# Two of four query and key projections moved behind the values and behind the base linear, each pair with its own tiles for the natural layout

## The reference

```
xn = layernorm(x)
q = (xn @ Wq.T + bq)      # 32 heads of 16, per head 1024 x 16
k = (xn @ Wk.T + bk)
v = (xn @ Wv.T + bv)
att = softmax(causal(q @ k.T / 4))
attn_out = (att @ v) @ Wo.T + bo
base_out = xn @ base_W.T + base_b
w = expert weights from softmax(xn @ router_W.T + router_b), mapped by expert_map
lora = ((xn @ A.T) * w) @ B * 2
x = x + attn_out + base_out + lora
```

## Time and profile before

| | us |
|---|---|
| median of three runs | 685.1 |
| lowest and highest | 684.2 to 689.15 |
| the profiled execution, its time | 686.73 |
| the profiled execution, its span | 685.0 |
| TensorE busy in it | 622.2 (91%) |
| DVE, ACT busy | 373.4, 293.7 |
| router logits to values, stretch | 266.15 to 334.73 |
| values, stretch | 334.73 to 371.42 |
| linear, up to the first score of attention | 371.42 to 416.64 |

### The profile page before, as it was taken

One profiled execution on the slowest core, in us unless ns is written; L12 is line 12 of the kernel. 1 busy time (PEld: TensorE's weight loads), 2 busy tenths in 40 slices (PEclk: granted clock), 3 DMA queues, 4 the chain that ended last, 5 costly groups with the idle time before them and its releaser, 6 DMA issues.

```text
span 685.0 us, 9336 instructions
## 1 busy us (share of the span) xinstructions
PE 622.2 (91%) x3688; PEld 407.8 (60%) x3688; DVE 373.4 (55%) x547; ACT 293.7 (43%) x509; POOL 76.9 (11%) x106
## 2 busy tenths in 40 slices
PE   3999999999999998872998997999999999989985
PEld 3788888878888866662765664444444444333444
DVE  6676553176453275431476546678888888610025
ACT  4545333135332132121321114677777777583450
POOL 3000000000000029000000232121221211211010
PEclk9999999999999999997899997999999999795998
DMA  6332332111101111478731003253362601010003
GB/s 217 124 103 93 113 104 81 61 38 56 61 32 61 62 62 25 145 191 217 266 110 31 2 1 68 41 107 78 60 108 46 96 25 29 12 31 10 11 26 127
DMA packets 24305, 53.64 MB, mean 78 GB/s; under 512 B 8881, under 2 KB 9393, under 8 KB 24257
## 3 DMA queue, kind: packets, MB, share of 16 engines
q1 hardware_dynamic: 23972, 52.46, 28.2%
q0 software_dynamic: 288, 0.58, 0.5%
HBM read 39.77 MB, written 10.61 MB: 74 GB/s over the span
## 4 chain that ended last, share of the span: by engine, by line
PE 74%; DVE 9%; ACT 7%; DMA 6%; issue 2%; SPq 1%; POOLq 0%; POOL 0%; ACTq 0%; DVEq 0%
PE bank L1148 11%; PE bank L1131 10%; PE slot L887 8%; PE bank L887 8%; PE bank L889 7%; PE bank L888 7%; PE slot L888 7%; PE slot L889 7%; DMA heads_dram<-attn_lo 6%; PE slot L1054 5%; ACT probs L869 5%; DVE maxcol L1453 2%; PE slot L1062 2%; DMA stage<-in_stream 1%; PE slot L903 1%
## 5 line engine op out<-in xcount | busy, mean ns | idle before, releaser
L869 ACT ACTIVATE probs<-bank 128x512 f32<-128x512 f32 (+2 forms) x320 | 156.1, 560 | 70.3 <-PE bank L1131 68.6
L1453 DVE TENSOR_REDUCE maxcol<-slot 128x2 f32<-128x1024 f32 (+2 forms) x112 | 124.8, 1142 | 42.7 <-PE slot L1062 22.3
L887 PE MATMUL slot<-xt_hi,ring_hi 128*128 128x512 f32 (+2 forms) x248 | 99.9, 403 | 21.7 <-DVE attn_lo L1409 18.2
L889 PE MATMUL slot<-xt_hi,ring_lo 128*128 128x512 f32 (+2 forms) x248 | 98.8, 399 | 0.0
L888 PE MATMUL slot<-xt_lo,ring_hi 128*128 128x512 f32 (+2 forms) x248 | 98.7, 398 | 0.0
L1148 PE MATMUL bank<-probs,v_sb 128*32 128x512 f32 (+3 forms) x768 | 90.6, 547 | 0.6 <-POOL probs L687 0.6
L1131 PE MATMUL bank<-qst,kst 50*128 50x512 f32 (+3 forms) x288 | 79.2, 440 | 7.5 <-ACT probs L869 6.5
L1131 PEld LDWEIGHTS bank<-qst,kst 50*128 50x128 f32 x288 | 36.4, 199 | 70.9 <-ACT probs L869 62.6
L887 PEld LDWEIGHTS slot<-xt_hi,ring_hi 128*128 128x128 f32 (+2 forms) x248 | 47.8, 193 | 34.5 <-issue 21.2
L687 POOL TENSOR_SCALAR_AFFINE_SELECT probs<-probs 128x512 f32<-128x512 f32 x64 | 41.7, 652 | 202.4 <-ACT probs L869 202.4
L1054 PE MATMUL slot<-kst,qst 48*128 48x512 f32 (+3 forms) x288 | 56.9, 388 | 7.7 <-DVE maxcol L1453 7.6
(11 more groups left out here) (185 smaller groups left out, 885.1 us busy)
## 6 DMA issues: line engine op xcount, KB each, us to landing
stage<-in_stream SPq DMA_DIRECT2D x43, 512.0 KB, 3.4
heads_dram<-attn_hi SPq DMA_DIRECT2D x8, 512.0 KB
heads_dram<-attn_lo SPq DMA_DIRECT2D x8, 512.0 KB
qst<-heads_dram SPq DMA_DIRECT2D x12, 256.0 KB, 5.9
kst<-heads_dram SPq DMA_DIRECT2D x12, 256.0 KB, 10.7
stage<-u_sb SPq DMA_DIRECT2D x68, 32.0 KB, 2.0
out_y<-x_sb SPq DMA_DIRECT2D x8, 256.0 KB, 2.2
stage<-den_dram SPq DMA_DIRECT2D x15, 128.0 KB
```

The source lines that it names most:

```text
L869: act.activation(probs[:, to:to + heads, 0:n], bank[b % 3][:, 0:heads * n].rearrange("p (h n) -> p h n", n=n), ACT.Exp, scale=HD ** -0.5). ...
L887: pe.matmul(out_ap, a[0], b[0], start=start, stop=False)
L889: return pe.matmul(out_ap, a[1], b[0], start=False, stop=stop)
L1453: dve.tensor_reduce(per_head[:, :, slots[0]:slots[-1] + 1], scores, AX.X, ALU.max).then_inc(S["max_free"], 1)
```

## The change

The items are reordered to qk0, qk1, lora1, wv0, wv1, qk2, base0, base1, qk3, wo0, wo1. TensorE makes q and k of m = 0 and 1 before the expert products as before, those of m = 2 between `values` and `linear`, and those of m = 3 between `linear` and attention. The natural layout has two sets: m = 1 and 3 keep the rows of attn_hi and attn_lo, m = 0 and 2 use the third part of qst and kst (`natural`), which is free until `stack(2)`. `project_hi(which, m)` so waits for the store of m-2. hw1 (the weighted expert products) gets tiles of its own, since "qk3" no longer leaves its ring half. GpSimd clears two stacks instead of three and adds the bias rows to x one by one behind `values(t)`. The DMA scratch shrinks from 8192 to 2048 bytes; it is room in memory, and the same DMAs are made.

```diff
-    for m in range(KD):
-        add("ring", f"qk{m}")
+    add("ring", "qk0")
+    add("ring", "qk1")
     add("ring", "lora1")
     for n in range(2):
         add(f"v{n}", f"wv{n}")
+    add("ring", "qk2")
     for n in range(2):
         add(f"base{n}", f"base{n}")
+    add("ring", "qk3")
...
-    users += [("r", 0)] + [(which, m) for m in range(KD) for which in ("q", "k")]
+    users += [("r", 0)] + [(which, m) for m in range(2) for which in ("q", "k")]
     users += [("a", 0), ("w", 0)]
     for g in range(2):
-        users += [("max", UNITS * g + u) for u in range(UNITS)] + [("m", g)]
+        users += [("max", UNITS * g + u) for u in range(UNITS)] + [("q", 2 + g), ("m", g), ("k", 2 + g)]
...
+        def natural(which, m, part):
+            if m % 2:
+                return (attn_hi, attn_lo)[part][:, 2 + "qk".index(which), :]
+            return (qst, kst)["qk".index(which)][:, 2, part, :]
...
-            for m, name in enumerate(("lora1", "wv0", "wv1", "base0")):
-                store("q", m)
-                store("k", m)
-                weights(item_at[(name, 0)])
-                if m in (1, 2):
-                    stack(m - 1)
+            store("q", 0)
+            store("k", 0)
+            weights(item_at[("lora1", 0)])
+            weights(item_at[("wv0", 0)])
+            stack(0)
+            weights(item_at[("wv1", 0)])
+            store("q", 1)
+            store("k", 1)
+            weights(item_at[("qk2", 0)])
+            stack(1)
+            weights(item_at[("base0", 0)])
             weights(item_at[("base1", 0)])
+            store("q", 2)
+            store("k", 2)
+            weights(item_at[("qk3", 0)])
+            neg_max(0)
             stack(2)
-            for name in ("wo0", "wo1"):
-                weights(item_at[(name, 0)])
-            neg_max(0)
+            weights(item_at[("wo0", 0)])
+            store("q", 3)
+            store("k", 3)
+            weights(item_at[("wo1", 0)])
             neg_max(1)
...
             for t in range(NT):
+                pool.wait_ge(S["v_done"], t + 1)
                 pool.tensor_tensor(x_sb[:, t, :], x_sb[:, t, :], bo_bc, ALU.add).then_inc(S["y_biased"], 1)
...
-                if m >= 1:
-                    act.wait_ge(S[f"{which}_stored"], 32 * m)
+                if m >= 2:
+                    act.wait_ge(S[f"{which}_stored"], 32 * (m - 1))
+                if m == 3:
+                    act.wait_ge(S["y_done"], NT)
...
             project_hi("k", 0)
-            for m, names in enumerate((["qk2"], ["qk3"], ["lora1", "wv0"]), 1):
-                for name in names:
-                    split_hi(item_at[(name, 0)])
-                project_hi("q", m)
-                project_hi("k", m)
+            split_hi(item_at[("lora1", 0)])
+            split_hi(item_at[("wv0", 0)])
+            project_hi("q", 1)
+            project_hi("k", 1)
             split_hi(item_at[("wv1", 0)])
...
+            split_hi(item_at[("qk2", 0)])
             act.wait_ge(S["w_free"], 1)
...
+            project_hi("q", 2)
+            project_hi("k", 2)
+            split_hi(item_at[("qk3", 0)])
             for t in range(NT):
                 act.wait_ge(S["y_done"], t + 1)
...
+            project("q", 2)
+            turn_maxima(0)
+            project("k", 2)
...
             for t in range(NT):
                 linear(t)
+            project("q", 3)
             turn_maxima(1)
+            project("k", 3)
...
+            project_lo("q", 2)
             negate_max(0)
+            project_lo("k", 2)
+            split_lo(item_at[("qk3", 0)])
             for u in range(UNITS, 2 * UNITS):
                 row_max(u)
+            project_lo("q", 3)
             negate_max(1)
+            project_lo("k", 3)
```

More of the change, by code:

```diff
@@ L360, in build @@
         u_sb = sb(block1, "u_sb", [P, 2, HALF])
+        hw1 = [sb(block1, f"hw1_{n}", [P, TOK], F32R) for n in ("hi", "lo")]
         den = sb(block1, "den", [P, 2, DEN_COLS])
@@ L462, in ring_of @@
             return n, ring_hi[:, r, :], ring_lo[:, r, :]
-        hw1 = ring_of(f"qk{KD - 1}")[1:]
         def ring_done(r):
@@ L518, in _ @@
             sp.dma_start(x_sb[:, 4:8, :], x_in[4:8].rearrange("t p d -> p t d")).then_inc(S["x_landed3"], 16)
-            for n in range(2, item_at[("qk3", 0)] + 1):
+            for n in range(2, item_at[("qk1", 0)] + 1):
                 weights(n)
@@ L526, in stack @@
                     sp.wait_ge(S["st_ready"], banks_before(g - STACKS + 1, 0))
-                if g < STACKS - 1:
+                if g < 2:
                     sp.wait_ge(S["blank"], g + 1)
+                if g == 2:
+                    for which in "qk":
+                        sp.wait_ge(S[f"{which}_stored"], 32 * 3)
                 if g == STACKS - 1:
-                    sp.wait_ge(S["y_done"], NT)
+                    sp.wait_ge(S["k_ready"], KD)
+                if 2 <= g < STACKS:
                     for side in range(2):
@@ L669, in _ @@
             pool.wait_ge(S["xn_ready"], 2 * NT)
-            for g in range(STACKS - 1):
+            for g in range(2):
                 pool.memset(keys(g).rearrange("p b n -> p (b n)").bitcast(F32), 1.0).then_inc(S["blank"], 1)
@@ L1027, in _ @@
             last.then_inc(S["lt_ready"], 1)
-            project("k", 0)
-            for m in range(1, KD):
-                project("q", m)
-                project("k", m)
+            for m, which in ((0, "k"), (1, "q"), (1, "k")):
+                project(which, m)
             pe.wait_ge(S["w_lo"], item_at[("lora1", 0)] + 1)
@@ L1428, in _ @@
             spread(gate_x1, gate, NT)
-            project_lo("k", 0)
-            for m, names in enumerate((["qk2"], ["qk3"], ["lora1", "wv0"]), 1):
-                for name in names:
-                    split_lo(item_at[(name, 0)])
-                project_lo("q", m)
-                project_lo("k", m)
+            split_lo(item_at[("lora1", 0)])
+            split_lo(item_at[("wv0", 0)])
+            project_lo("q", 1)
+            project_lo("k", 1)
             split_lo(item_at[("wv1", 0)])
@@ L1439, in _ @@
                               ).then_inc(S["w_free"], 1)
+            split_lo(item_at[("qk2", 0)])
             dve.wait_ge(S["hw_hi_ready"], 3)
-            dve.tensor_tensor(hw1[1], hw_f1, hw1[0].bitcast(F32), ALU.subtract
+            dve.tensor_tensor(hw1[1][:], hw_f1, hw1[0][:].bitcast(F32), ALU.subtract
                               ).then_inc(S["hw1_ready"], 1)
```

34 lines of the change are left out of this document (18 added, 16 removed).

## The result

The changed kernel takes **723.9 us** in the median of four runs (716.0 to 731.8), the kernel before 687.1 in four runs on the same chip (684.2 to 689.2). The ratio is **1.048, 95% interval 1.043 to 1.054**, so about 33 us are lost.

The account below looks back on a forecast made before the run. TensorE, busy 622.2 of 685.0 us, was taken as the bound, with time only where it idles or runs slowly. The terms -18.0 + 13.2 + 12.6 + 11.2 + 12 = +31 took the median 685.1 to 716 us, range 699 to 731.

Parts of the forecast that it names:

- Part 1: Up to the values: scores that stood at 343.47 come at 323.5; lead 20.0, less 2.0 for slow clock, 18.0 gained.
- the wait before "a": Ahead of the expert products: TensorE idles some 9 us while lora1 and wv0 are loaded and split.
- The sum by volume: Second estimate of qk2's landing: 5.6 MB from 286 on at 204 GB/s, 27.5 us, so 313.5.
- Part 2: Between values and linear: two projections, 10.8, plus a slot wait of 2.4 cost 13.2, leaving a lead of 4.8.
- Part 3: In linear: qk3, loaded behind a store, stops TensorE; a lead of 4.8 becomes a lag of 7.8, costing 12.6.
- Part 4: Between linear and attention: q and k of m = 3 add 10.9 and 0.3, bringing the lag to 19.0.
- Part 5: In attention's first exponentials: wo1, loaded behind a store, lands about 14.5 after issue; ACT stands 12.2, costing 12.
- At nothing: base0: In the values: base0 and base1 land near 323 to 325, DVE needs base0 near 328, so no cost.
- (a): Rival: every load lands 3.3 us behind its issue, as with an empty queue; 13 gained, 672 us; chance 0.08.
- (b): Rival: stores drain faster with gaps between them, loads take some 7 us; +12, 697 us; chance 0.18.
- (c): Rival: store of m = 1 held by stack 0, base0 stops DVE, wo1 takes 21.2; 731 us; chance 0.08.
- The price from the Trainium skill's Bandwidth section: Stores: 1 MB in 6.15 us would make the sum about +9, 694 us; set aside as measured from HBM to SBUF.

Follow-up runs that it names:

- e12: Changed kernel with the loads of lora1 and wv0 issued at the start, ahead of the stores of m = 0 and the first stack: 714.9 us, ratio 1.037.
- e3: Changed kernel with the load of qk3 issued ahead of the stores of m = 2: 713.5 us, ratio 1.034.
- e11: Changed kernel with the load of wo1 alone issued ahead of the store of m = 3: 708.7 us, ratio 1.032.
- e2: Changed kernel with the load of qk2 issued ahead of the stores of m = 1: 721.9 us, ratio 1.052.
- e4: Changed kernel with the loads of qk2, qk3 and wo1 each ahead of the stores beside them: 695.2 us, ratio 1.011.
- e6: Changed kernel with wide stores (destination 128 x 1024 instead of 8 x 16 x 1024), loads still behind the stores: 703.9 us, ratio 1.019.
- e10: Changed kernel with wide stores, lora1, wv0, wv1, qk2, qk3 and wo1 loaded earlier and base items split later: 675.3 us, ratio 0.983.
- e9: Kernel before with the wide stores alone, one set of tiles and nothing moved: 667.5 us, ratio 0.968.

## Why the prediction held, and where its steps were off

The sign and the mechanism are as predicted: 716 with 699 to 731, measured 723.9. It is the likeliest case, with the sum at 33 (by the ratio) to 37 (by the medians) instead of 31.

**Part 1, up to the values: right, with a wrong inside.** The lead at the scores was predicted 18.0 with the clock, and is 18.8; the first maximum was put at 320.5 and is at 320.46. The landing of qk2, taken as 317 between 313 and 321, lets ACT split at 317.10. But the wait before "a" is 13.9, not some 9: lora1 is split at 291.32 and wv0 at 295.27, not from 288 and 289 on. The stack's read, issued from 281.87 on, and the store of k were under way at the same time, which I take for the reason without a run that shows it, and the store went out at 276.68, not at 274.9. This wait set the time when the stores of m = 1 went out, and so when qk2 could come: the first at 298.81, not at 293. That 317 was met all the same is in part luck. qk2 was issued at 302.70 where my sequence had it near 298, and it landed 14.4 us behind its issue, not 21.2; the two errors cancel. TensorE's two waits, 13.9 and 7.0, are 20.9 together as I had them (9, and 12 from 309 to 321), but I had put them elsewhere. e12 shows what the first one was worth: 8 us by the ratio. The sum by volume has a slip as well: the transfers named are 5.8 MB, not 5.6, which gives 314.3 instead of 313.5, within the ends.

**Part 2, q and k of m = 2: the step that was mis-sized.** 13.2 was predicted, 17.8 measured (from -18.8 to -1.0). The slot wait is there with 2.51 for 2.4. What I hadn't put in is that each of the two projections runs partly at half clock: q takes 7.1 us for its 24 matmuls (353.34 to 360.47) and k as much (363.25 to 370.39), where I had 5.4, and the windows above give 0.69 for both starts, 17 matmuls in 5.5 us. Together that is 3.4 of the 4.6. It isn't the same in every execution: in the profiles of the changed kernel and its seven variants (e2, e3, e4, e6, e10, e11, e12) q takes 7.1 in four and 5.5 in four, and k 7.0 to 7.2 in seven and 5.5 in one (e2). TensorE comes to both from a stretch with waits: the maxima's pace before q, the slot before k. I had charged 2.0 for the clock behind each of two long stops and nothing behind a short one.

**Part 3, qk3: right.** From -1.0 to +11.2 is 12.2, predicted 12.6; the load was split 11.3 us after its issue, predicted 11.6 and the maxima behind it. e3 takes it away and gets 10 back.

**Part 4, q and k of m = 3: right.** 11.8 (from 11.2 to 23.0), predicted 11.2; the slot wait is 2.50.

**Part 5, wo1: the stop nearly right, its tail too small.** The load came 12.1 after its issue instead of 14.5, and ACT stood 10.17, not 12.2. The lag still grew by 13.0 up to the first inversion, since the stretch runs at half clock; e11, without the stop, gets 12 back by the ratio and 15 by the medians. In the profiled execution the slow stretch goes on beyond 490 and costs 8 more.

**At nothing: base0.** Right in the changed kernel (its split waits 5.3 us for the load at 325.35, and TensorE's next waits are at most 1.1), and wrong as soon as qk2 comes earlier: 2.8 us in e2. The prediction named that cover.

**The rivals.** (a), loads as with an empty queue, is out: the three loads that it rests on (qk2, qk3, wo1) landed 14.4, 11.3 and 12.1 us behind their issue. (b), half of it, is what wide stores make (e6: 703.9 against 697), so its premise, that a store drains faster, is the right lever, but not with this layout. (c) put more loss into later loads; but wo1 landed 12.1 us behind its issue, not 21.2, and base0 stopped nothing, so what came above my sum came mostly through the clock. The price from the Trainium skill's Bandwidth section (1 MB in 6.15 us), which gave 694, doesn't fit this store at 11.7; the wide one takes 4.2, less than that price. Both go from SBUF to HBM, so the direction, which I had named as the reason for the 11.7, isn't it; the layout of the destination is.

## What to carry to other kernels

When a wait on a buffer goes, look at what else is queued behind the transfer that held it: here the loads that SP issued right behind a store of the old shape landed 11 to 21 us behind their issue, and a second buffer moved the wait to the next such load. Two things helped. The loads put ahead of the stores gave back 26 of the 33 us that the change lost (e4). And asking why the transfer is slow: 11.7 us for 1 MB went with a destination whose slowest dimension is 8, and laying out the scratch array anew gave 3.2% on the kernel before, with nothing moved, where two sets of tiles gave 1.8% (intervals 2.7 to 3.8% and 0.1 to 3.6%, so their order isn't shown). Last, a gap in TensorE's work is to be priced with the slow stretch beside it: k of m = 2, behind a slot wait of 2.5 us, took some 1.6 us longer in seven of eight profiles than in the eighth.

## What was unexpected in the hardware

**The layout of a store's destination changes its price by a factor of 2.4 and more**: 1 MB alone takes 10.2 us as 8 x 16 rows and 4.2 as 128 rows, at a DMA share of 0.48 against 0.88 in the stretches shown; beside other transfers it is 11.7 against 4.2.

**The clock carries part of every stop, and varies between executions of one kernel.** The four runs of the changed kernel take 716.0, 722.9, 725.0 and 731.8 us at mean granted clocks of 0.930, 0.923, 0.913 and 0.899, the two levels being mixed differently; the kernel before stands at 0.94 to 0.96 in all but one of its executions (0.928), and e9 at 0.96 to 0.97. By the trace's clock records the slow stretch around the stop for wo1 lasted from 442.6 to 497.3 in the profiled execution of the changed kernel, 55 us; around the same stop in e2, e3 and e12 it lasted 31 us each (441.4 to 472.2, 432.9 to 463.6, 432.6 to 463.3). What decides its length stays open here.
